# Two batches that take turns on each group of head weights, in a gated cross-attention block

## The reference

```python
ln_out = _ln(hidden_states, ln_w, ln_b)
q = _fp8_linear_pertensor(ln_out, wq, wq_scale, q_in_scale)      # 16 heads of 128
q = _ln(q, qln_w, qln_b)                                         # the same for k (8 groups), qx, kx
v = _fp8_linear_pertensor(ln_out, wv, wv_scale, v_in_scale)
core = _gqa(q, k, v)                                             # softmax(q k^T) v over x
kvx = cond @ w_kv_x.T                                            # kx, vx from the context
xout = _gqa(qx, kx, vx)
cat = concat([core, xout]); catq = _div_clamp_fp8(cat, proj_smooth)
x = x + tanh(g_xattn) * (catq @ wproj.T) * (proj_in_scale * proj_w_scale)
# feed-forward: weights clip(round(w / mean|w|), -1, 1) * mean|w|, activations to 8 bit per row
x = x + tanh(g_ffn) * bitlinear(silu(a) * b, w_down),  a, b = bitlinear(layernorm(x), w_gate_up)
```

## Time and profile before

| | us |
|---|---|
| median of 3 runs | 2003.69 |
| lowest, highest | 1998.87, 2005.06 |
| profiled execution, own time | 2004.23 |
| profiled execution, span | 2002.4 |

### The profile page before, as it was taken

One profiled execution on the slowest core, in us unless ns is written; L12 is line 12 of the kernel. 1 busy time (PEld: TensorE's weight loads), 2 busy tenths in 40 slices (PEclk: granted clock), 3 DMA queues, 4 the chain that ended last, 5 costly groups with the idle time before them and its releaser, 6 DMA issues.

```text
span 2002.4 us, 35210 instructions
## 1 busy us (share of the span) xinstructions
PE 1668.2 (83%) x11147; PEld 1013.2 (51%) x11164; DVE 1746.9 (87%) x4062; ACT 1188.1 (59%) x2963; POOL 1017.8 (51%) x1327
## 2 busy tenths in 40 slices
PE   1467777768899998989999777999999958999996
PEld 0344444445566665556666444555566623444442
DVE  5769989999999989999999999999999955777774
ACT  2025556546788886778797656677777851222222
POOL 3476666666766665676665455555666521000000
PEclk7678999898999999999999999999999978999997
DMA  2236666767999998889999878899998797333200
GB/s 86 84 119 148 145 150 133 171 151 175 197 225 195 211 227 185 179 191 226 202 204 197 183 173 180 191 212 214 209 188 163 135 237 242 88 92 88 74 17 16
DMA packets 664285, 325.48 MB, mean 163 GB/s; under 512 B 551328, under 2 KB 594464, under 8 KB 663072
## 3 DMA queue, kind: packets, MB, share of 16 engines
q1 hardware_dynamic: 664096, 323.17, 71.6%
HBM read 140.61 MB, written 48.23 MB: 94 GB/s over the span
## 4 chain that ended last, share of the span: by engine, by line
DVE 50%; PE 27%; POOL 9%; issue 7%; DMA 3%; ACT 3%; SPq 0%; POOLq 0%; DVEq 0%; ACTq 0%
DVE pp L948 9%; DVE nmx L938 9%; PE psum L687 5%; PE psum L662 5%; PE psum L645 4%; PE psum L633 3%; PE psum L605 3%; PE psum L704 3%; DVE xh L921 3%; DVE wbt L826 2%; DMA pt<-pp 2%; PE psum L612 2%; POOL raw L1353 2%; DVE cc L962 2%; DVE ast L907 2%
## 5 line engine op out<-in xcount | busy, mean ns | idle before, releaser
L633 PE MATMUL psum<-qk 128*128 128x512 f16 x1536 | 427.7, 388 | 74.5 <-DVE pp L948 71.1
L605 PE MATMUL psum<-wbt,xqt 128*128 128x256 f16 (+1 forms) x4096 | 413.8, 251 | 53.6 <-DVE xh L921 39.7
L1236 ACT ACTIVATE psum<-psum,nmx 128x512 f32<-128x512 f32 x512 | 341.1, 666 | 143.6 <-DVE nmx L938 139.3
L605 PEld LDWEIGHTS psum<-wbt,xqt 128*128 128x128 f16 x4096 | 334.5, 100 | 167.3 <-DVE xh L921 45.2
L948 DVE SCALAR_TENSOR_TENSOR pp<-psum,prs,pp 128x512 f16<-128x512 f32 x512 | 377.8, 738 | 16.5 <-ACT pp L1247 16.5
L1247 ACT ACTIVATE pp<-psum,prs 128x512 f16<-128x512 f32 x512 | 351.2, 686 | 20.9 <-DMA pt<-pp 20.9
L938 DVE TENSOR_REDUCE nmx<-psum 128x1 f32<-128x512 f32 x512 | 342.8, 670 | 17.9 <-PE psum L633 17.2
L1242 ACT ACTIVATE prs<-psm 128x1 f32<-128x1 f32 x512 | 108.1, 211 | 258.7 <-DVE psm L943 257.3
L1429 POOL TENSOR_TENSOR qk<-y,qk 128x512 f16<-128x512 f32 x192 | 233.7, 1217 | 16.0
L633 PEld LDWEIGHTS psum<-qk 128*128 128x128 f16 x1536 | 142.8, 99 | 166.2 <-DVE pp L948 79.8
L645 PE MATMUL psum<-pt,vx 128*128 128x512 f16 x768 | 203.3, 389 | 24.5 <-ACT cy L1255 21.5
(11 more groups left out here) (169 smaller groups left out, 2801.6 us busy)
## 6 DMA issues: line engine op xcount, KB each, us to landing
wbt<-ws SPq DMA_DIRECT2D x192, 256.0 KB, 3.6
ws<-wbt SPq DMA_DIRECT2D x64, 256.0 KB, 3.9
catd<-cy SPq DMA_DIRECT2D x64, 256.0 KB, 3.3
raw<-in_wgu SPq DMA_DIRECT2D x64, 256.0 KB, 3.6
wbt<-catd SPq DMA_DIRECT2D x8, 2048.0 KB, 9.8
raw<-in_w SPq DMA_DIRECT2D x32, 384.0 KB, 3.8
pt<-pp SPq DMA_TRANSPOSE x512, 3.5
raw<-in_wp SPq DMA_DIRECT2D x32, 256.0 KB, 3.7
```

The costliest lines, as they stand in the source:

```text
L605: ins = e.matmul(bank[:, o0:o0 + c1 - c0], xv[:, v, kt * 512 + tt * 128:kt * 512 + (tt + 1) * 128], wb[i][:, h, kt, c0:c1], start=kt == 0 ...
L633: ins = e.matmul(SB(n), qk[i][:, jq, u, ss], qk[i][:, jk, w, :], start=k == 0, stop=k == 2)
L1236: e.activation(SB(n), SB(n), ACT.Exp, bias=nmx[:, k], accum_out=psm[:, k]).then_inc(s["exp"], 1)
```

## The change

- A step is now one group for one of two batches in turn: steps 0 to 15 are groups 0 to 7, each for batch 0 and then batch 1; steps 16 to 31 are groups 7 to 0, each for batches 2 and 3 (`place`). Weights of a group stay in their half of wbt for two steps, and groups 6 and 7 stay there over the turn, so six groups are stored (48 pieces) and loaded once (48 pieces). The preparation of a group takes the same instructions, and stands every 32 slots.
- x and context of batch 1 are prepared ahead of slot 0, those of batch 2 in slots 4 to 108 and of batch 3 in 118 to 222, into a tile xs and from there to memory (xd, cd); they come back when batches 0 and 1 are done with their buffers.
- Group factors: four POOL instructions a step in place of five on DVE.
- Both high halves of v are one ACT instruction, both low halves one DVE instruction (tile vv, 128x256).
- Late weights: the sums are 24 pieces of 128x1024, loaded and summed by ACT before slot 0, in the space of qk's second buffer; splits and ternary pieces run from slot 234, one in 35/12 slots, through four buffers in xs. A ternary piece is one instruction each on POOL, DVE and ACT. The high half of the projection weight goes to memory too (wpd) and is loaded in the last eight slots.
- The loads for the projection and the feed-forward block are cut in pieces, one a slot.

```diff
+def place(it):
+
+    stage, i = divmod(it, 2 * NG)
+    return 2 * stage + i % 2, NG - 1 - i // 2 if stage else i // 2
...
-        it, j = divmod(n - PREP_HI[kt] + 2 * SLOTS, SLOTS)
-        if j == 0 and 0 < it < NG:
-            out.append((it, kt))
+        g, j = divmod(n - PREP_HI[kt], 2 * SLOTS)
+        if j == 0 and 0 < g < NG:
+            out.append((g, kt))
...
-PREP_HI = (-10, -6, -4, -1)
+PREP_HI = (-54, -48, -42, -36)
...
-JOBS_FROM, TERN_FROM = 92, 309
-SCALE_AT = {"sum": 303, "whole": 308, "fac": 310}
+JOBS_FROM = 234
+SCALE_AT = {"sum": -6, "whole": -3, "fac": -1}
...
+JOB_AT = {JOBS_FROM + m * 35 // 12: m for m in range(len(JOBS))}
...
-            def load_w(it, k):
+            def load_w(p, k):
+
+                _, g = place(2 * p)
                 cols = slice(k * 1024, (k + 1) * 1024)
-                q.wait_ge("gb", (it - 1) * 4)
-                q.wait_ge(f"w_st{it % 2}", 128 * (NG // 2))
-                e.dma_start(wbt[:, it % 2, cols], ws[it % NG][:, cols]).then_inc(s[f"w_ld{it % 2}"], 16)
+                q.wait_ge("gb", 8 * (p - 1))
+                q.wait_ge(f"w_st{g % 2}", 128 * (NG // 2 - 1))
+                e.dma_start(wbt[:, g % 2, cols], ws[g][:, cols]).then_inc(s[f"w_ld{g % 2}"], 16)
...
+            def load_wp(c):
+                q.wait_ge("hd_tr", NIT * 6)
+                q.wait_ge("gb", NIT * 4)
+                e.dma_start(wps[:, 4 * c:4 * c + 4, :], wpd[:, 4 * c:4 * c + 4, 0:512]).then_inc(s["wp_ld"], 16)
...
+            def load_sum(c):
+
+                src, j = SUMS[c]
+                q.wait_ge("l_sum", c - 2)
+                e.dma_start(sumb[c % 3].rearrange("p (c n) -> p c n", c=2), late_src[src][:, j:j + 2, :]
+                            ).then_inc(s[f"su_ld{c % 3}"], 16)
+
+            def early_sum(c):
+                f = sumb[c % 3]
+                q.wait_ge(f"su_ld{c % 3}", 16 * (c // 3 + 1))
+                e.activation(f, f, ACT.Abs, accum_out=wsum[:, c:c + 1]).then_inc(s["l_sum"], 1)
+                if c + 2 < len(SUMS):
+                    load_sum(c + 2)
...
+                q.wait_ge("o_y", (it - 3) * 4)
+                e.tensor_scalar(f[:, 0:1], cmx[:, b, 1:2], wmx[:, g, 1:2], 2.0 ** -20, ALU.mult, ALU.mult)
+                q.done(e.tensor_scalar(f[:, 1:2], cfa[:, b:b + 1], wfa[:, g:g + 1], 1.0, ALU.mult, ALU.mult))
+                e.tensor_scalar(eps6[it % 4][:, 5:6], f[:, 1:2], f[:, 1:2], EPS * D, ALU.mult, ALU.mult)
+                e.tensor_scalar(f[:, 2:4], aco[:, 16 + 2 * g:18 + 2 * g], f[:, 0:1], 8.0,
+                                ALU.mult, ALU.mult).then_inc(s["gf"], 1)
...
-                e.scalar_tensor_tensor(vs[ix][:, tt, 1, :], bank[:, 128:256], VSCALE, vs[ix][:, tt, 0, :],
-                                       ALU.mult, ALU.subtract)
-                e.scalar_tensor_tensor(vx[ix][:, tt, 1, :], bank[:, 384:512], XSCALE, vx[ix][:, tt, 0, :],
-                                       ALU.mult, ALU.subtract).then_inc(s["vx_lo"], 1)
+                e.scalar_tensor_tensor(vv[ix][:, tt, 1], bank.rearrange("p (a b) -> p a b", a=2)[:, :, 128:256], VSCALE,
+                                       vv[ix][:, tt, 0], ALU.mult, ALU.subtract).then_inc(s["vx_lo"], 1)
```

More of the change, by code:

```diff
@@ L22 @@
 NHC = NIT * 4
[L23 to L24 removed]
+VSCALE = 2.0 ** -14
 PSCALE = 2.0 ** 11
@@ L37 @@
 FACTORS_AT = 7
-PREP_HI = (-10, -6, -4, -1)
-KV_AT = {"part": 2, "spread": 3, "whole": 4, "fac": 5, "hi": 5, "lo": 6}
+PREP_HI = (-54, -48, -42, -36)
+KV_AT = {"part": -33, "spread": -32, "whole": -31, "fac": -30, "hi": -30, "lo": -29}
 OUT_AT = {"clip": 17, "field": 18, "step": 19, "add": 20, "sub": (21, 23), "store": 26}
-JOBS_FROM, TERN_FROM = 92, 309
-SCALE_AT = {"sum": 303, "whole": 308, "fac": 310}
-FLAG_AT = {"sum": 306, "whole": 324, "fac": 326}
+JOBS_FROM = 234
+SCALE_AT = {"sum": -6, "whole": -3, "fac": -1}
+FLAG_AT = {"sum": 330, "whole": 334, "fac": 336}
+W_AT, XD_AT, CD_AT = -54, 104, 108
+CAT_AT, WG_AT, X2_AT, WP_AT = (-54, -24), (-40, -19), -14, -8
+BACK_AT = {2: 218, 3: 234}
+X_FROM = {2: 4, 3: 118}
+X1_AT = {
+    "quant": tuple(range(-28, -8)),
+    "bound": (-27, -26, -25, -24),
+    "cxp": (-23,),
+    "cxs": (-22,),
+    "cxw": (-21,),
+    "cxf": (-19,),
+    "parts": (-17, -16, -15, -14),
+}
 X_AT = {
@@ L83, in prep_at @@
     for kt in range(4):
-        it, j = divmod(n - PREP_HI[kt] + 2 * SLOTS, SLOTS)
-        if j == 0 and 0 < it < NG:
-            out.append((it, kt))
+        g, j = divmod(n - PREP_HI[kt], 2 * SLOTS)
+        if j == 0 and 0 < g < NG:
+            out.append((g, kt))
     return out
 def kv_at(n, what):
-    it, j = divmod(n - KV_AT[what] + 2 * SLOTS, SLOTS)
-    return [it] if j == 0 and 0 < it < NG else []
+    g, j = divmod(n - KV_AT[what], 2 * SLOTS)
+    return [g] if j == 0 and 0 < g < NG else []
 def x_steps(n, what):
[L98 to L101, removed]
+    out = [(1, t) for t, when in enumerate(X1_AT.get(what, ())) if when == n]
+    for b in (2, 3):
+        out += [(b, t) for t, when in enumerate(X_AT[what]) if X_FROM[b] + when == n]
+    return out
 def out_at(n):
@@ L155, in job_tables @@
         up(f"raw_ld{k % 2}", k)
[L156 to L174, removed]
+    for m, (what, _, _) in enumerate(JOBS):
+        for name in (f"j_ld{m % 4}", f"l_st{m % 4}") + (("l_hi", "l_lo", "l_ab") if what == "split" else
+                                                      ("l_t0", "l_t1", "l_t2")):
+            up(name, m)
+    return value
+JV = job_tables()
 def ring_tables():
@@ L447, in sp_program @@
             load_x(0)
-            for kt in range(4):
-                load_raw(0, kt)
+            load_raw(0, 0)
+            load_raw(0, 1)
+            load_x(1)
+            load_ctx(1)
+            load_raw(0, 2)
+            load_raw(0, 3)
             load_ctx(0)
@@ L705, in down @@
                 ins.then_inc(s["dn"], 1)
-            for kt in range(4):
-                x_turn(0, kt)
+            for b in range(2):
+                for kt in range(4):
+                    x_turn(b, kt)
             w_whole(0)
@@ L1106, in dve_program @@
                 head_means(0, kt)
+                if kt == 0:
+                    for t in range(4):
+                        x_stats(1, t)
                 prep_w(0, kt)
+                if kt == 2:
+                    for t in range(4):
+                        x_norm(1, t)
             for col, v in ((0, 0), (1, 0), (2, 1), (3, 1), (4, 2)):
@@ L1273, in act_program @@
                     x_turned(0, kt, v)
+            for c in range(4):
+                early_sum(c)
+            for kt in range(4):
+                for v in range(4):
+                    x_turned(1, kt, v)
+            for c in range(4, 12):
+                early_sum(c)
             q.wait_ge("pre_w", 1)
```

401 lines of the change are left out of this document (212 added, 189 removed).

## The result

The changed kernel takes 2038.88 us (median of 4 runs, 2035.23 to 2040.27), the kernel before 2001.4 us in the runs beside it. The ratio is 1.018, with a 95% interval of 1.016 to 1.021: slower by 37 us, where 92 us less was forecast.

What follows compares the result with a forecast made beforehand. VectorE was taken as the bound wherever it has side work, TensorE elsewhere. Stages 141 + 693 + 678 + 398.6 gave 1911 us of span, with 1.8 around it; prediction 1912 us, 4.6% faster, range 1862 to 1955.

Steps and rivals of the forecast that it cites:

- What bounds the kernel; the floor: Main loop: VectorE bounds slots with side work, TensorE bare ones at 2.447 us; ternary slots forecast at 2.49 us.
- Part 1: Main loop: group factors leave VectorE for GpSimd, which has room; saves VectorE 1.65 us a step, 0.10 a slot.
- Part 2: Ternary blocks of late weights: VectorE's three instructions, 1.26 us a block, become one of 0.5; GpSimd scales and clips.
- Part 3: Head-weight preparation: not made smaller, only spaced 32 slots apart; 11 us of VectorE work moves from prologue into the loop.
- with the same share: Slots 0 to 224: 656 us of VectorE work with 5.3% of the time as holes, giving 693 us.
- Part 4: Prologue: second batch's x and context add 31 us of VectorE work, half hidden in 47 us of waits; slot 0 at 141.
- Part 5: Main loop: two low parts of v become one instruction, saving 0.05 us for each of 128 tiles, 6 us.
- Part 6: Prologue: 48 sums become 24 double ones on ScalarE; 47 us of sums against 45 us of room, costing 2 us.
- The rival on the slow side: Prologue: sums delay ScalarE's first copy of v, eating the whole gain from 7.7 us a sum; 2008 at 8 us; chance 0.03.
- Tail: Slot 496 to the end: no change from 398.6 us, bounds 15 less and 15 more.
- The lock: Ternary slots: GpSimd's new instructions block VectorE through shared ports every time, 48 us, 38 after cover; 1949 us; chance 0.10.
- moved work that lands on covered time: Whole kernel: on-chip weight reuse is hidden and the moved work gains nothing, so the result is 2000 us; chance 0.02.

Runs made afterwards that it cites:

- e11: Changed kernel, ternary minimum moved to VectorE, context weights' steps three slots later, later half of side jobs one slot later, factors in slots 7 and 4 alternately: 1943.9 us.
- e3: Changed kernel with the group factors put back on VectorE as five instructions: 2039.3 us, ratio 1.019.
- e2: Changed kernel with GpSimd's group factors in slot 4 of each 16 in place of slot 7: 2024.8 us, ratio 1.012.
- e1: Changed kernel with the ternary minimum moved from GpSimd to VectorE; GpSimd multiplies and adds the rounding constant instead: 1994.9 us, ratio 0.996.
- e5: Changed kernel with the six steps of the context projection's weights three slots later: 2015.1 us, ratio 1.007.
- e10: Changed kernel without 16 of the 20 instructions that quantize the second batch's x ahead of slot 0: 2030.5 us, ratio 1.014.
- e7: Changed kernel with the copy and the low part of v each done by two instructions again: 2042.6 us, ratio 1.020.
- e4: Changed kernel without the 24 sums and their 12 MB of loads, weight scales taken from a constant: 2037.2 us, ratio 1.018.
- e12: e11 with two of the four weight preparation parts moved by two slots each: 1958.8 us, ratio 0.978.
- e13: Changed kernel, minimum left on GpSimd, with VectorE's and ScalarE's part of each side job, its store and next load one slot later: 2010.7 us.
- e14: Changed kernel with the edits of e1, e5 and e13 together and the group factors in slot 6: 1952.7 us, ratio 0.976.

## Why the prediction was wrong, point by point

- *What bounds the kernel; the floor.* Right in the main. Slots 464 to 480, bare as slots 448 to 480 were, take 2.49 us (2.447 before), e11's ternary slots 2.51; e11's own bare slots take 2.40 with TensorE busy for 99%, so the floor is some 2% lower than forecast. The last 16 slots, "as now, 33.2", took 37.5, which no run explains.
- *Part 1, factors to GpSimd.* Failed: "so it has room". Its work was right (four instructions, 1.4 us), its place was never looked at: they stand ahead of a result that VectorE waits for. e3: worth nothing where it was put. e2: 14 us back by another slot.
- *Part 2, ternary blocks.* VectorE's one operation was right (0.5 taken, 0.43 median, 0.6 mean). The failed step is the one that has no number: "POOL scales and clips". I priced VectorE's end of the hand-over, between two rows of the trace, and put GpSimd's end at nothing, without a row and without a bound. It measured 2.00 us a block, 44 us in all (e1).
- *Part 3, preparation.* Its work was right (the sum of 656 stands at 657.7). That the tables also decide who shares a PSUM bank with whom was not seen: "with the same share" of holes, 5.3%, is the step that failed. It was 11.3%. The 5.3% was too low even for the kernel before: it came from my sum of 677 us for VectorE's work there, which the trace has at 668.0, so 6.6%, and 702 us for the changed kernel in place of 693. The later place of the context weights' steps gives 24 us of the 48 that slots 0 to 224 were too long (e5), the factors' place 14 (e2, alone).
- *Part 4, the second batch in the prologue.* "Half of the work gained falls into the 47 us": the work was 106 (110 forecast), but 47 us of waits stayed. 12 us too low, inside its bounds of 130 to 157 (its own terms make 142, not 141). For the quantization 4 in 10 were hidden (e10); the rest is argued from the chain, not tried: the second batch's statistics and GpSimd's factors for them stand ahead of the first preparation.
- *Part 5, v.* 0.14 us saved each; 3.7 us in time, not clear of noise (e7), 6 forecast.
- *Part 6, sums.* The 2 us were about right: nothing (e4). The rival on the slow side put its weight on the one thing that cost nothing.
- *Tail.* 392.8 us, 6 under the forecast.
- *The lock.* VectorE's ternary operation has a median of 0.43, a mean of 0.61 and a most of 1.37 us. 17 of the 48 take over 0.5 us; at the start of each a 128x512 instruction of GpSimd was running (L1487 or L1500), and VectorE's ended 0.28 us after it. The other 31 met only tiny instructions of GpSimd, or none. 48 times the mean less the least (0.41) is about 10 us, not 48. The rule of the Trainium skill (SBUF — State Buffer, "Who interferes with whom") is borne out by these rows, but it was not the cause: e1, 44 us faster, has 17 as well.

The sum: 127 us between 1912 and 2038.9. Minimum 44, later place of the context weights' steps 24, and lag and place of the factors 27 (e11 in all 95); 32 stay. By e11's profile, taken of a slower execution, 42 stay: 13 in the prologue, 22 in slots 0 to 224, 10 in slots 224 to 496, 3 less behind. Why slots 0 to 224 still hold 59 us of waits there is open: slot 11 of each 32 has the longest (1.5 us in the mean), behind the preparation on GpSimd, and e12 only moved it. The lag of e13 mends in part what e1 mends, so its 28 us and e1's 44 do not add up.

A slower kernel had a chance of 0.04. What the prediction named for a gain that comes to nothing was sums that hold up the prologue and moved work that lands on covered time; no rival held GpSimd's new operation, the queue behind the factors or the ring.

## What to carry to other kernels

When work is moved to an engine "with room", price it there, by an instruction with the same operations, and then look at what is queued behind it and who waits for that: the mean utilisation told neither here. When a table of slots is changed, look at every resource that is handed out in program order (here three PSUM banks) and count the uses with a short distance, before and after. Where the buffers allow it, try a hand-over between engines one slot later: here it gave 28 us (e13) and 14 (e14).

## What the runs showed of the hardware that was not expected

- GpSimd, 128x512 fp32, scale from memory: multiply and minimum 2.00 us (least 1.99), multiply and add 0.69, multiply twice (to fp16) 0.62. VectorE's step with the minimum and the maximum (e1): 0.43.
- A VectorE instruction on 128x512 fp32 in SBUF, 0.41 to 0.43 us, took 0.84 or 1.37 us in the changed kernel when a 128x512 instruction of GpSimd was running at its start (17 of 17), and no longer than usual beside GpSimd's instructions on 128x2 and 128x4.
- 12 MB of extra loads beside the prologue's own (DMA share 0.45 against 0.21) did not move slot 0.
